# The first layer norm taken batch by batch, with three of its four batches moved in among the first turn's preparations

## What is computed

```python
mu = jnp.mean(x, axis=-1, keepdims=True)
var = jnp.mean(jnp.square(x - mu), axis=-1, keepdims=True)
xn = (x - mu) * jax.lax.rsqrt(var + LN_EPS) * gamma       # x: (4, 1024, 128)
q = (xn @ w_q)                                            # 16 heads of 64
k, v = jnp.split(xn @ w_kv, 2, axis=-1)
...
q = _l2norm(q) * q_scale
k = _l2norm(k) * k_scale
sim = jnp.einsum('bhid,bhjd->bhij', q, k) * ATTN_SCALE    # + a slope per head, causal
out = jnp.einsum('bhij,bhjd->bhid', jax.nn.softmax(sim), v)
```

## Time and profile before

| | us |
|---|---|
| median of 3 runs | 1969.05 (1968.14 to 1970.12) |
| the profiled execution, its own time | 1974.28 |
| its span in the profile | 1972.5 |
| first use of the rows, DVE L139 | 12.67 |
| first projection of turn 0, PE L381 | 45.27 |
| first scores of turn 0, PE L486 | 88.05 |

### The profile page before, as it was taken

How to read it: one execution, slowest core, us unless ns; L and a number is a source line. 1 busy time by engine, 2 the same in 40 slices (tenths; PEclk the granted TensorE clock), 3 DMA queues, 4 the chain that set the end, 5 groups by cost and what they waited for, 6 DMA issues and landing times. The chain is left out here.

```text
span 1972.5 us, 28814 instructions
## 1 busy us (share of the span) xinstructions
PE 1632.6 (83%) x8973; PEld 766.2 (39%) x8974; DVE 1096.6 (56%) x2591; ACT 760.9 (39%) x1253; POOL 562.7 (29%) x557
## 2 busy tenths in 40 slices
PE   2699999999999999999999999844973777776777
PEld 1244444444444444443444444443651332232332
DVE  4246556546556655655655655562225666667664
ACT  2345444454454454454454454302431322322221
POOL 1342442442532533533533533152002011110000
PEclk9799999999999999999999999956995887887788
DMA  5501021020220220220220200041110000000000
GB/s 169 159 1 59 16 73 49 25 73 12 62 73 4 70 73 1 73 73 1 73 73 1 73 4 1 1 156 43 47 41 12 6 11 11 11 11 6 0 6 11
DMA packets 109361, 82.02 MB, mean 42 GB/s; under 512 B 5601, under 2 KB 101113, under 8 KB 108974
## 3 DMA queue, kind: packets, MB, share of 16 engines
q1 hardware_dynamic: 107182, 76.15, 12.6%
q0 software_dynamic: 2048, 4.20, 0.7%
HBM read 31.57 MB, written 48.76 MB: 41 GB/s over the span
## 5 line engine op out<-in xcount | busy, mean ns | idle before, releaser
L689 ACT ACTIVATE P<-S,keyb 128x386 f32<-128x386 f32 (+7 forms) x512 | 296.3, 629 | 414.3 <-PE S L490 403.4
L486 PE MATMUL S<-QT,KT 64*128 64x512 f32 (+5 forms) x1792 | 373.1, 473 | 12.7 <-DVE KT L816 11.0
L992 POOL TENSOR_TENSOR rn<-nm,half 128x12 f32<-128x12 f32 x128 | 323.8, 2539 | 23.6 <-DVE nm L753 23.6
L851 DVE TENSOR_TENSOR Psum<-Psum,P 128x1796 f32<-128x1796 f32 (+7 forms) x256 | 287.8, 1124 | 36.2 <-PE O L510 18.4
L1008 POOL TENSOR_SCALAR_AFFINE_SELECT P<-P 128x256 f32<-128x256 f32 (+1 forms) x256 | 117.2, 458 | 620.4 <-ACT P L689 620.3
L510 PE MATMUL O<-P,V 128*64 128x512 f32 (+5 forms) x1536 | 256.7, 437 | 13.9 <-POOL P L1008 11.8
L486 PEld LDWEIGHTS S<-QT,KT 64*128 64x128 f32 (+1 forms) x1792 | 156.5, 178 | 202.9 <-issue 194.0
L162 POOL TENSOR_TENSOR norm_rstd<-norm_vareps,half 128x4 f32<-128x4 f32 x40 | 40.9, 1023 | 481.5 <-DVE norm_vareps L147 481.4
L381 PE MATMUL W<-xT,wts 128*128 128x512 f32 x256 | 142.8, 653 | 15.0 <-DVE QT L812 7.2
L490 PE MATMUL S<-GQ,GK 64*128 64x512 bf16 (+5 forms) x896 | 148.7, 301 | 0.0
L873 DVE TENSOR_TENSOR part<-W,rden 128x512 f32<-128x512 f32 x128 | 82.2, 683 | 91.0 <-PE W L558 91.0
(11 more groups left out here) (214 smaller groups left out, 2221.2 us busy)
## 6 DMA issues: line engine op xcount, KB each, us to landing
xg<-zero SPq DMA_DIRECT2D x16, 1216.0 KB, 8.9
yg<-zero SPq DMA_DIRECT2D x16, 1216.0 KB, 11.9
xT<-xnt SPq DMA_DIRECT2D x16, 512.0 KB, 4.6
wts<-in_w_qkv SPq DMA_DIRECT2D x16, 384.0 KB, 5.6
gu<-in_gu SPq DMA_DIRECT2D x1, 2816.0 KB, 10.3
xb<-xg SPq DMA_DIRECT2D x40, 64.0 KB, 1.8
yg<-yb SPq DMA_DIRECT2D x40, 64.0 KB, 1.6
X<-in_x SPq DMA_DIRECT2D x8, 256.0 KB, 4.5
```

Source lines behind the costliest of these rows:

```text
L486: nc.tensor.matmul(S[hh][0:m, at + c:at + c + w], KT[d, r, p, jt * P:jt * P + m], QT[d, r, p, Q0[jt] + c:Q0[jt] + c + w], start=True, stop ...
L689: nc.scalar.activation(probs(p, jt)[0:m, hh, 0:n], S[hh][0:m, at:at + n], ACT.Exp, bias=keyb[0:m, r, (2 * p + hh) * NKT + jt:(2 * p + hh) ...
L851: nc.vector.tensor_tensor(x, x, probs(p, jt)[0:m, :, 0:NQ[jt]], ALU.add).then_inc(add_ok, 1)
L992: nc.gpsimd.tensor_tensor(rn[:, c, u], nm[:, c, u], powers, ALU.pow).then_inc(rn_ok, 1)
```

## The change

- The pieces become halves of one batch: `half_of(h)` is four chunks of batch h // 2. SyncE loads `X` in four transfers, one for each batch, with a semaphore each: batch 0 first, batch 1 after five small constants, batches 2 and 3 after all constants. Turn 0's `wt` is loaded fourth in the queue.
- The first norm has its own statistics tiles with eight slots (`first = Norm("first", TT)`).
- Halves 0 and 1 are normalised at once, and ACT writes them straight into `xT`. Halves 2 and 3 (batch 1) also go straight into `xT`, into its second slot. Halves 4 to 7 still go through `xnst` and the DRAM tensor.
- `xT` has a slot for each of two batches in place of two turns: it is loaded from DRAM twice (after turns 3 and 7) instead of 16 times.
- DVE takes the statistics of halves 2 to 7 right behind the null keys and before `w1m`.
- PE does the null keys' transpose and the two small products behind lap 2 of turn 0's preparation instead of before lap 0.
- The rest of halves 2 to 7 stands between laps: DVE's `vector_apply` after laps 4, 9 and 13, PE's transposes after laps 6, 9 and 13, ACT's scaling after laps 7, 10 and 14, two halves each time. PE waits for all eight before turn 0.
- SyncE's loops are written out; its first clears stand behind the stores of halves 4 to 7.

```diff
+        first = Norm("first", TT)
...
+            AHEAD = 4
+            AT_LAPS = {6: (2, 3), 9: (4, 5), 13: (6, 7)}
+            DVE_LAPS = {4: (2, 3), 9: (4, 5), 13: (6, 7)}
+            ACT_LAPS = {7: (2, 3), 10: (4, 5), 14: (6, 7)}
+            def half_of(h):
+                return X[:, 4 * (h % 2):4 * (h % 2) + 4, h // 2, :]
...
+                load_batch(0)
                 sp.dma_start(idf[:], a["c_idf"]).then_inc(ld_f, 16)
                 sp.dma_start(gam[:], a["gamma"]).then_inc(ld_f, 16)
-                for c in range(TT):
-                    sp.dma_start(X[:, c], a["x"][:, c]).then_inc(ld_x, 16)
+                load_weights(0, 0)
...
+                load_batch(1)
...
+                load_batch(2)
+                load_batch(3)
+                load_weights(1, 1)
...
+                for h in range(AHEAD, TT):
+                    sp.wait_ge(xnt_ok, h + 1)
+                    sp.dma_start(xnt[:, h // 2, 4 * (h % 2):4 * (h % 2) + 4, :], xnst[:, h % 2]).then_inc(st_xn[h % 2], 16)
                 sp.wait_ge(zero_ok, 1)
                 clear(TURNS - 2)
                 clear(TURNS - 1)
...
+                    load_weights(t + 2, r)
+                    if t in (NG - 1, 2 * NG - 1):
+                        load_rows(t // NG + 2)
...
+                turned(0)
+                turned(1)
                 for s in range(STEPS + 1):
                     prepare(0, 0, 0, f"{s}a", True)
                     prepare(0, 0, 0, f"{s}b", True)
+                    if s == 2:
+                        pe.wait_ge(ld_c, LDC)
+                        pe.wait_ge(ld_w, LDW)
+                        pe.wait_ge(null_k, 1)
...
+                    for h in AT_LAPS.get(s, ()):
+                        turned(h)
+                pe.wait_ge(xnt_ok, TT)
                 turn(0, 0, 0, True)
...
+                dve.wait_ge(ld_x[0], 16)
+                for h in range(2):
+                    first.vector_stats(dve, half_of(h), h)
+                for h in range(2):
+                    first.vector_apply(dve, half_of(h), xns0[h], h)
                 dve.wait_ge(ld_c, LDC)
                 dve.wait_ge(ld_w, LDW)
...
+                for h in range(2, TT):
+                    if h % 2 == 0:
+                        dve.wait_ge(ld_x[h // 2], 16)
+                    first.vector_stats(dve, half_of(h), h)
                 dve.wait_ge(g_mm, 1)
                 nc.vector.tensor_tensor(w1m[:], S[0][:, 0:D], blk[:], ALU.mult).then_inc(g_ok, 1)
...
+                    for h in DVE_LAPS.get(s, ()):
+                        dve.wait_ge(xnt_mm, h - 1)
+                        hold(dve)
+                        first.vector_apply(dve, half_of(h), xns0[h % 2], h)
```

More of the change, by code:

```diff
@@ L227, in build @@
             W = [ps(f"W{i}", [P, 512], F32, sc) for i in range(2)]
-            ld_x, ld_w, ld_c, ld_f = s1("ld_x"), s1("ld_w"), s1("ld_c"), s1("ld_f")
+            ld_x, ld_w, ld_c, ld_f = [s1(f"ld_x{b}") for b in range(NB)], s1("ld_w"), s1("ld_c"), s1("ld_f")
             ld_xw, ld_wo = [s1(f"ld_xw{i}") for i in range(2)], [s1(f"ld_wo{i}") for i in range(2)]
@@ L297, in _, with load_batch, load_rows, load_weights @@
             def _(sp):
-                credit(sp, st_xn)
-                sp.dma_start(idf[:], a["c_idf"]).then_inc(ld_f, 16)
-                sp.dma_start(gam[:], a["gamma"]).then_inc(ld_f, 16)
-                for c in range(TT):
-                    sp.dma_start(X[:, c], a["x"][:, c]).then_inc(ld_x, 16)
[L303 to L323, removed]
+                def load_batch(b):
+                    sp.dma_start(X[:, :, b, :], a["x"][:, :, b, :]).then_inc(ld_x[b], 16)
+                def load_rows(b):
+                    sp.dma_start(xT[:, b % 2, NNULL:NKEY].rearrange("p (c n) -> p c n", n=P), xnt[:, b]).then_inc(ld_rows, 16)
+                def load_weights(n, r):
                     sp.dma_start(wt[:, r, :], a["w_qkv"][:, bass.ds(n % NG, 1), :].rearrange("p a n -> p (a n)")).then_inc(ld_xw[r], 16)
@@ L341, in _ @@
                 clear(TURNS - 1)
[L342 to L349, removed]
+                for r in range(2):
+                    sp.wait_ge(st_xn[r], 16 * (TT - AHEAD) // 2)
+                for t in range(TURNS - 2):
+                    r = t % 2
+                    sp.wait_ge(prep_mm, prepared(t, ROOTS[0]))
+                    load_weights(t + 2, r)
+                    if t in (NG - 1, 2 * NG - 1):
+                        load_rows(t // NG + 2)
+                    clear(t)
+                    sp.wait_ge(out_mm, formed(t, 1, 5))
+                    load_out(t + 2, r)
             LDC, LDW = 16 * 11, 16 * 6
@@ L408, in vals @@
                         jt = 2 * j + i
-                        last = nc.tensor.matmul(o, xT[:, r, jt * P:(jt + 1) * P], wt[:, r, 2 * KW:], start=True, stop=jt > 0)
+                        last = nc.tensor.matmul(o, xT[:, n // NG % 2, jt * P:(jt + 1) * P], wt[:, r, 2 * KW:], start=True, stop=jt > 0)
                         if jt == 0:
@@ L434, in roots @@
                     if c == 0:
-                        last = nc.tensor.matmul(W[BANK[k]][0:NNULL, KW:2 * KW], xT[:, r, SEQ:NKEY], wt[:, r, 2 * KW:], start=True, stop=True)
+                        last = nc.tensor.matmul(W[BANK[k]][0:NNULL, KW:2 * KW], xT[:, n // NG % 2, SEQ:NKEY], wt[:, r, 2 * KW:], start=True, stop=True)
                     last.then_inc(prep_mm, 1)
@@ L596, in finish, with turned @@
                     outputs(t, r, 0, 1, 1, False)
-                pe.wait_ge(ld_f, 32)
[L599 to L618, removed]
+                def turned(h):
+                    pe.wait_ge(first.done, h + 1)
+                    if h >= 2:
+                        pe.wait_ge(xnt_ok, h - 1)
+                    for b in range(NB):
+                        last = nc.tensor.transpose(S[h % 2][:, b * P:(b + 1) * P], xns0[h % 2][:, b, :], idf[:])
+                    last.then_inc(xnt_mm, 1)
+                pe.wait_ge(ld_f, 32)
+                turned(0)
+                turned(1)
                 for s in range(STEPS + 1):
@@ L630, in _ @@
             def _(act):
-                credit(act, xnt_ok, ot_ok)
+                credit(act, ot_ok)
                 act.sem_inc(exp_ok, 2 * STEPS)
@@ L709, in turn, with settled @@
                             pair_out(t, 0)
-                act.wait_ge(ld_f, 32)
[L712 to L722, removed]
+                def settled(h):
+                    act.wait_ge(xnt_mm, h + 1)
+                    if h < AHEAD:
+                        at = NNULL + 512 * (h % 2)
+                        to = xT[:, h // 2, at:at + 512].rearrange("p (b n) -> p b n", b=NB)
+                    else:
+                        to = xnst[:, h % 2]
+                        if h >= AHEAD + 2:
+                            act.wait_ge(st_xn[h % 2], 16 * ((h - AHEAD) // 2))
+                    nc.scalar.activation(to, S[h % 2][:, 0:CH].rearrange("p (b n) -> p b n", b=NB), ACT.Copy,
+                                         scale=gam[:, 0:1]).then_inc(xnt_ok, 1)
+                act.wait_ge(ld_f, 32)
+                settled(0)
+                settled(1)
                 for s in range(STEPS):
                     prepare(0, 0, s)
+                    if s == 2:
+                        act.wait_ge(null_t, 1)
+                        src = O[:, 0:H * NNULL].rearrange("p (g h k) -> p g h k", g=2 * NG, h=2)
+                        for hh in range(2):
+                            nc.scalar.copy(nkT[hh * DH:(hh + 1) * DH], src[hh * DH:(hh + 1) * DH, :, hh, :]).then_inc(null_te, 1)
+                    for h in ACT_LAPS.get(s, ()):
+                        settled(h)
                 turn(0, 0, True)
@@ L937, in _ @@
                 nc.vector.memset(xT[:, :, 0:NNULL], 0.0).then_inc(consts, 1)
[L939 to L943, removed]
-                    hold(dve)
-                    for r in range(2):
-                        first[r].vector_apply(dve, chunk(X, 2 * i + r), xns0[r], i)
+                dve.wait_ge(ld_x[0], 16)
[3 more added lines that the diff above has]
+                    first.vector_apply(dve, half_of(h), xns0[h], h)
                 dve.wait_ge(ld_c, LDC)
@@ L1021, in _ @@
                 pool.wait_ge(consts, 1)
-                with pool.Fori(0, TT // 2) as i:
-                    for r in range(2):
-                        first[r].pool(pool, i)
+                for h in range(2):
+                    first.pool(pool, h)
                 pool.wait_ge(null_ss, 3)
                 nc.gpsimd.tensor_tensor(nkss[:, 1:2], nkss[:, 0:1], half[0:H * NNULL, 0, 0:1], ALU.pow).then_inc(null_rn, 1)
+                for h in range(2, TT):
+                    first.pool(pool, h)
                 pool.wait_ge(ld_c, LDC)
```

61 lines of the change are left out of this document (42 added, 19 removed).

## The result

The changed kernel took 1963.34 us in the median of 13 runs (1954.47 to 1964.47), the kernel before 1971.79 us in as many runs of the same kind (1966.19 to 1979.21). The ratio is 0.9943, 95% interval 0.9924 to 0.9962: faster by 0.6%, some 11 us by the ratio and 8.5 by the two medians, where 21 were forecast. The time is 15.3 us above the forecast of 1948.05 and outside the range of 1943 to 1955. The profiled execution took 1963.62, with a span of 1961.9, against 1974.28 and 1972.5.

What follows compares the result with a forecast made beforehand. The opening, 88.05 us before the first scores, was taken as the price ahead of a dense block: N0 26.5 us earlier less 5.5 for insertions gives 21.0 off 1969.05, so 1948.05 us, range 1943 to 1955 (8 in 10).

Steps and rivals of the forecast that it cites:

- N0: PE product in turn 0's preparation, behind the first projections: to start at 27.15 instead of 53.61, 26.5 us earlier.
- the wait named: Before N0, PE waits for DVE's w1m and w1q, late through constants (14.6) and six halves' statistics (9.0 us).
- The rows' side: Loading and normalising X, then the first projections: would allow N0 at 22.4, 4.7 us before the deciding constants' side.
- The insertions: Norm work put between laps from N0 to the first scores: 1.3 + 0.8 + 3.4 = 5.5 us, bounds 3.5 and 9.
- the same mix of slow and fast: PE's clock in the changed preparation taken as before, adding nothing: 1948; with the stall slowing it, 1951.
- The paragraph on the clock: If the projections behind N0 ran slow altogether, eight at about 0.9 us more each, some hidden: some 3 us later.
- lap 6: Eight PE transposes inserted in turn 0's preparation behind N0, on the path: 1.3 us, bound 2.2.
- E1: PE step of turn 0's preparation, behind lap 13's insertions and before the first scores: 3.4 us of waiting, expected at 61.8.
- laps 9 and 13: DVE applies and PE's last transposes before the first scores: 0.8 us comes through at lap 9, 3.4 at lap 13.
- Provided that the turns behind it run as before: Condition that the attention's 16 turns keep their length, so each us off the opening comes off the total.
- the first scores: End of turn 0's preparation, start of the dense attention block: forecast at 67.1 instead of 88.05, 21.0 us earlier.
- dips in the turns: Rival, 4%: the 1.6 us dip could strike each shifted turn; from 13 turns on 1969 or more.

Runs made afterwards that it cites:

- the second pair of profiles: Changed kernel and kernel before, both run again unaltered: 1957.92 us, ratio 0.9923, and 1972.67 us, ratio 0.9998.
- the delayed kernel before: Kernel before with four DVE memsets added late in turn 0's preparation, so the turns start later: 1979.85 us, ratio 1.0048.
- filled: Either kernel with products of zeros in PE's two idle places of each turn with a preparation: changed 1951.38 us (0.9883), before 1968.88 us (0.9981).

## Why the prediction was wrong

**N0 (forecast 27.15, measured 27.02).** Right, in time and in reason: the wait named was the one that ended last, and moving three us of statistics moved it. X landed at 5.1, a little under my 6.0, at no gain, as said. The rows' side was ready at about the forecast time by luck: P00 came at 12.60 and not at 14.0, but P00 to P03 took 8.3 us and not 6.45, as P02 and P03 ran at the slow rate (3.78 us for four matmuls, 1.98 before), though the profile has the granted clock at 1.00 there; it records the half clock only from 24.3 on.

**The insertions (forecast 5.5, measured 6.8).** N0 to the scores is 41.21 against 34.44 (88.05 - 53.61) before. The first powers come 4.45 us behind N0 instead of 3.75, because N0 itself was 0.9 us longer (1.94 against 1.06): the granted clock was 0.50 from 24.3, in the 4.4 us wait, to 37.9. That is the term I had set at nothing in the main sum by taking the same mix of slow and fast. (The paragraph on the clock counts eight projections between N0 and V0; there are four, and its 3 us fit four.) From the first powers to the second, where lap 6 stands, the road is 1.2 longer (1.3 reckoned), and from the second powers to E1 4.8 longer (17.12 against 12.30), for laps 9 and 13 (4.2 reckoned). With their applies and transposes out of E0's and E1's way, 3.9 came back. In the second pair of profiles the road is 39.63 against 33.25, 6.4.

**"Provided that the turns behind it run as before".** This is the step that failed: the path behind the first scores, taken as fixed in length. It was in the first paragraph as a condition and in the sum as a fact: I took the block of 1135 us as fixed and even let the median be free of its 3.2 us. It is not fixed. It is 1131.2 to 1131.8 with every dip gone, and 1133 to 1145 in the unfilled profiles of either kernel. The change does nothing to its content, but in the profiled execution it was 9.15 us longer, and that is most of the miss in the span: 10.6 us gained at the end, where 19.8 were gained at the first scores. In the medians 15.3 us are missing: 2.7 because the kernel before is at 1971.79 in thirteen runs and not at the 1969.05 of three, and 12.6 because 8.45 of 21.0 arrived. What stands behind the block I took as fixed as well: 692.5 to 695.8 us in the three profiles of the kernel before, 696.2 in the two of the changed one.

**The rival "dips in the turns".** I named the mechanism and mis-sized it. I made it all or nothing, 13 turns or more, with 4%, and left out everything between. The rows showed two dips in one execution; from one execution I could not know how many the next has, and three runs within 2 us of each other were too few: the larger samples run from 1965 to 1979 on one chip. With samples of that size beforehand the range would have had to reach some 5 us or more further up. The Trainium skill (TensorE: Matmul & The Clock Gate, What's actually happening) says that the monitor of the clock runs free of the kernel; the three profiles of one program with one, two and seven disturbed turns agree with that. I drew the wrong end from it, that the draws are alike. From one execution to the next they are not, and by the delayed kernel before they may not be pure chance either.

**What of the gap is shown.** Unfilled against filled, side by side: the changed kernel gains 6.5 us in the median by the filler (1957.92 to 1951.38), the kernel before 2.2 (1971.13 to 1968.88). Filled against filled the change is worth 17.5. So 4 us of the missing ones are the clock in the turns, which struck the changed kernel harder in that set of runs (of 6 and 4 runs, so roughly). The 19.8 at the first scores is itself the difference of one pair: in the filled pair it is 17.5 (86.02 against 68.55). The openings of an unchanged program differ by such amounts: between 88.05 and 86.02 X is usable 0.6 us earlier and the road from N0 to the scores is 1.2 shorter, with the granted clock at half for 3.4 us behind N0 instead of 6.9. That the filled medians are 17.5 apart as well is in part luck, as the two filled profiles lie only 9.6 apart: the changed one lost 3.2 in the block, at turn 15, and 4.1 behind it. Whether the changed kernel draws more dips on average, or drew more here, is left open.

## What to carry to other kernels

A gain worked out in the opening can be real, as here at the first scores, and still not arrive at the end, if the block behind does not take the same time in every execution; look for stretches of equal work and unequal length in one profile, and take the profile of the same program two or three times before calling the block fixed. On a kernel that is dense on PE, a wait of 2 us that repeats in each turn costs more than its length now and then, and a few products of zeros in it can be cheaper than removing it. An insertion between laps costs what its last producer is late, not its own busy time: the same work put one or two laps earlier, under POOL's wait, cost 0.4 us between the end of the second powers and E1 instead of 4.7.

## What the runs showed of the hardware

The granted clock went to half for about 3.4 us, or twice that, in 23 of the 105 turns 0 to 14 of seven unfilled profiles, 21 times behind PE's 1.9 us wait and twice behind its 0.7 us wait. It did so in none of the 90 turns of six profiles in which 1.7 us of the long wait were filled. A dip of 3.4 us cost 1.6 us, one of 6.8 us 2.9 to 3.1. The same filler at a place where PE was busy left a dip in each of the first fifteen turns. Unaltered, the kernel before ran from 1964.90 to 1983.94 over all its runs here, on at least two chips, 1.0%, at one and the same program; on the chip of most experiments alone from 1964.90 to 1979.03, 0.7%.
